# Up projections of a feed-forward layer as three rounded matmuls, with weights split on the chip and streamed through a ring of four blocks

## What is computed

```python
x = _rmsnorm(src + sa, norm1_w)
flat = x.reshape(S, C)                                   # 4096 x 256 in all
shared = _swiglu(flat @ W_shared_in) @ W_shared_out      # W_shared_in: 256 x 1024
...
h = _swiglu(flat @ W1_shared)                            # W1_shared: 256 x 1024
routed = jnp.zeros_like(shared)
for e in range(E):                                       # 8 experts, 512 x 256 each
    routed = routed + h @ W2_experts[e] * w[:, e:e + 1]  # w: gates, top 2 of a group of 4
out = x + (shared + routed).reshape(Bb, Tt, C)
```

## Time and profile before

| | |
|---|---|
| runs, median of 3 | 2171.25 us (2167.96 to 2177.17) |
| profiled execution, its own time | 2162.3 us |
| span of its trace | 2160.3 us |
| PE busy | 1944.1 us (90%) |
| DVE busy | 1376.3 us (64%) |
| ACT busy | 824.8 us (38%) |
| POOL busy | 345.0 us (16%) |
| mean granted PE clock | 0.922 of 2.4 GHz |
| DMA, mean | 48 GB/s |

### The profile page before, as it was taken

How to read it: one execution, slowest core, us unless ns; L and a number is a source line. 1 busy time by engine, 2 the same in 40 slices (tenths; PEclk the granted TensorE clock), 3 DMA queues, 4 the chain that set the end, 5 groups by cost and what they waited for, 6 DMA issues and landing times.

```text
span 2160.3 us, 31763 instructions
## 1 busy us (share of the span) xinstructions
PE 1944.1 (90%) x9200; PEld 1039.4 (48%) x9200; DVE 1376.3 (64%) x4293; ACT 824.8 (38%) x1714; POOL 345.0 (16%) x647
## 2 busy tenths in 40 slices
PE   6868899999999999999999999999999989999896
PEld 4343445536364453645455353553635445364555
DVE  7457564766857476675767657675585856767354
ACT  2433534262433425244342543426243352533410
POOL 3224013101320014100131011310122001410000
PEclk9577889999998999999999898999999998999998
DMA  5004002110030102101021010311003010110302
GB/s 178 2 20 157 1 2 98 41 41 11 7 142 1 52 1 89 60 2 51 2 89 59 10 42 2 109 40 41 12 2 115 33 51 1 70 69 2 127 10 98
DMA packets 23089, 104.69 MB, mean 48 GB/s; under 512 B 3312, under 2 KB 14192, under 8 KB 18288
## 3 DMA queue, kind: packets, MB, share of 16 engines
q1 hardware_dynamic: 21168, 89.81, 11.4%
q0 software_dynamic: 1728, 12.58, 1.5%
HBM read 84.56 MB, written 16.78 MB: 47 GB/s over the span
## 4 chain that ended last, share of the span: by engine, by line
PE 64%; DVE 17%; issue 14%; ACT 3%; POOL 1%; DVEq 0%; DMA 0%; SPq 0%; ACTq 0%; POOLq 0%
PE fb L741 14%; PE fb L719 10%; PE ot L691 9%; PE sm L649 8%; PE st L677 4%; DVE negmax L1035 3%; PE dn L617 3%; PE st L617 2%; PE st L633 2%; PE sm L677 2%; DVE acc L1228 2%; DVE sm L1032 2%; PE dn L659 1%; PE ot L617 1%; PE dn L703 1%
## 5 line engine op out<-in xcount | busy, mean ns | idle before, releaser
L538 ACT ACTIVATE probs<-st 128x512 f32<-128x512 f32 (+3 forms) x832 | 397.7, 506 | 388.2 <-PE st L677 383.5
L741 PE MATMUL fb<-w_r,h_r 128*128 128x512 f32 x1536 | 451.0, 430 | 24.7 <-DVE acc L1228 13.3
L649 PE MATMUL sm<-k_t,q_t 48*128 48x512 f32 (+3 forms) x864 | 329.1, 469 | 69.1 <-DVE negmax L1032 28.5
L741 PEld LDWEIGHTS fb<-w_r,h_r 128*128 128x128 f32 x1536 | 282.3, 197 | 137.7 <-issue 69.7
L1035 DVE TENSOR_REDUCE negmax<-sm 128x1 f32<-128x512 f32 x416 | 270.3, 686 | 105.9 <-PE sm L649 105.6
L677 PE MATMUL st<-q_t,k_t 64*128 64x512 f32 (+3 forms) x832 | 310.3, 460 | 16.6 <-ACT probs L538 16.3
L649 PEld LDWEIGHTS sm<-k_t,q_t 48*128 48x128 f32 x864 | 148.3, 201 | 365.8 <-DVE negmax L1032 181.0
L719 PE MATMUL fb<-xn_t,wup_s 128*128 128x512 f32 x512 | 303.3, 691 | 2.2 <-DVE sg L1206 2.0
L1032 DVE CUSTOM_DVE_ANT_0 sm<-sm,mask_qk 128x384 f32<-128x384 f32 (+1 forms) x448 | 203.9, 463 | 140.2 <-PE sm L649 137.7
L691 PE MATMUL ot<-probs,v_s 128*32 128x512 f32 (+3 forms) x2048 | 254.7, 537 | 2.3 <-POOL probs L441 2.3
L402 POOL TENSOR_TENSOR stack<-rot,stack 128x256 fp32r<-128x256 f32 x64 | 49.6, 775 | 1089.9 <-ACT stack L474 1089.9
(11 more groups left out here) (163 smaller groups left out, 2450.0 us busy)
## 6 DMA issues: line engine op xcount, KB each, us to landing
w_r<-w_parts SPq DMA_DIRECT2D x32, 2048.0 KB, 7.9
w_parts<-w_r POOLq DMA_DIRECT2D x4, 2048.0 KB, 8.8
x_s<-in_L_attn_query SPq DMA_DIRECT2D x8, 512.0 KB, 4.9
h_s<-in_L_ffn_W_experts POOLq DMA_DIRECT2D x8, 512.0 KB, 6.0
q_t<-rot_b SPq DMA_DIRECT2D x256, 4.0 KB
x_kept<-o_s SPq DMA_DIRECT2D x8, 512.0 KB, 3.0
xa<-x_kept SPq DMA_DIRECT2D x8, 512.0 KB, 3.7
out<-acc SPq DMA_DIRECT2D x8, 512.0 KB, 12.8
```

The lines of the kernel that those rows point to most:

```text
L538: nc.scalar.activation(probs[:, n % PSLOTS, 0:hi - lo], score_bank(m)[:, 0:hi - lo], ACT.Exp, scale=float(D) ** -0.5).then_inc(s_ex, 1)
L649: mm(max_bank(w, a)[:, 0:hi - lo], q_t[r:r + MROW, b, t * P:(t + 1) * P], k_t[r:r + MROW, b, lo:hi], start=True, stop=True).then_inc(s_sm, 1)
L741: last = mm(fb[q % 2][:, :], h_r[:, h, m, rows], w2_r[:, k % 2, w, m, :], start=(m == 0 and n == 0), stop=(m == NH - 1 and n == 2))
```

## The change

The up projections take three rounded matmuls a step in place of one in fp32. The rows get a high part (a second copy by ACT, in `stack[:, 0]`, columns 0 to 31 of each of 32 rows) and a low part (GpSimd, in `stack[:, 1]`). The weights are split by GpSimd in batch 0, `w_si` after the first attention's masks, `w1` after the second attention's low parts, through `h_s` and `h_r`, and stored to DRAM; SP streams them back each batch in eight blocks of 512 KB through a ring of four. The splitting of the first pair of expert weights moves behind them. Two of SP's first loads (1 MB each) go.

```diff
-HIDDEN_AT = spread(8 * NH - len(QUIET), 6 - LEAD, 2) + QUIET
+HIDDEN_AT = spread(8 * NH - len(QUIET), 8 - LEAD, 3) + QUIET
...
+RING = 4
...
-        wup_s = sb("wup_s", [P, 2, NC, 2 * HID])
+        wup_r = sb("wup_r", [P, RING, 2, 2, NC, P], F32R)
...
+        xn_parts = [stack[:, w, :, 0:NC * D] for w in range(2)]
...
-                (wup_s[:, 0, :, :], w_si.rearrange("(c p) n -> p c n", p=P)),
-                (wup_s[:, 1, :, :], w1.rearrange("(c p) n -> p c n", p=P)),
...
-            def place_maxima(i, a):
+            def place_maxima(i, a, f=None):
...
+                    if f is not None:
+                        for n in ((4, 5), (6,), (7,), ())[g]:
+                            load_up(f, n)
...
+            def load_up(f, n):
+
+                if n >= RING or not isinstance(f, int) or f > 0:
+                    sp.wait_ge(s_ub, f * N_UB + n - RING + 1)
+                sp.dma_start(wup_r[:, n % RING].bitcast(F32), wup_parts[n]).then_inc(s_wu[n % RING], 16)
...
                 if more:
                     sp.dma_start(x_s[:, :, :], x_v[i + 1]).then_inc(s_x, 16)
                 if f is not None:
+                    for n in range(RING):
+                        load_up(i, n)
+                if f is not None:
                     load_pair(f, 2, e)
...
             batch(0, None, None, True)
+            sp.wait_ge(s_wup, 32)
+            for n in range(RING):
+                load_up(0, n)
             sp.wait_ge(s_w2p, 16 * PAIRS)
...
             x1_from_dram(B - 2)
+            for n in range(RING, 2 * NH):
+                load_up(B - 1, n)
             store(B - 2)
...
+            def split_up(u):
+
+                pool.wait_ge(s_wur, 16 * (u + 1))
+                if u > 0:
+                    pool.wait_ge(s_wup, 16 * u)
+                for c in range(NC):
+                    raw = wup_raw[:, c].rearrange("p (h n q) -> p n h q", h=2, n=NH)
+                    g.tensor_copy(wup_split[:, :, 0, :, c, :], raw).then_inc(s_wuh, 1)
+                pool.wait_ge(s_wuh, NC * (u + 1))
+                for c in range(NC):
+                    raw = wup_raw[:, c].rearrange("p (h n q) -> p n h q", h=2, n=NH)
+                    g.tensor_tensor(wup_split[:, :, 1, :, c, :], raw, wup_split[:, :, 0, :, c, :].bitcast(F32),
+                                    ALU.subtract).then_inc(s_wul, 1)
+                pool.wait_ge(s_wul, NC * (u + 1))
+                g.dma_start(wup_parts[u * NH:(u + 1) * NH].rearrange("n p w h c q -> p n (w h c q)"),
+                            wup_split.bitcast(F32).rearrange("p n w h c q -> p n (w h c q)")).then_inc(s_wup, 16)
+
+            def rows_low(f, stacks_done):
+
+                hi, lo = (x.rearrange("p h (c d) -> p c h d", c=NC) for x in xn_parts)
+                rows = xn_t[:, :, :].rearrange("p c (h d) -> p c h d", d=D)
+                pool.wait_ge(s_sp, stacks_done)
+                for c in range(NC):
+                    pool.wait_ge(s_xh, f * N_XH + c + 1)
+                    g.tensor_tensor(lo[:, c], rows[:, c], hi[:, c].bitcast(F32), ALU.subtract).then_inc(s_xl, 1)
+
+            load_up_raw(0)
+            low_parts(0, 0)
+            mask_probs(0, None)
+            split_up(0)
+            load_up_raw(1)
+            low_parts(0, 1)
+            split_up(1)
             load_raw(0)
             load_raw(1)
             split_pair(0)
-            low_parts(0, 0)
-            mask_probs(0, None)
-            low_parts(0, 1)
             split_pair(1)
             split_pair(2)
             split_pair(3)
             with pool.Fori(1, B) as i:
                 low_parts(i, 0)
+                rows_low(i - 1, i * N_SP + 16)
                 mask_probs(i, i - 1)
                 low_parts(i, 1)
+            rows_low(B - 1, B * N_SP)
...
-            def copy_expert_rows(f):
+            def copy_expert_rows(f, i):
+                if i is not None:
+                    act.wait_ge(s_sp, i * N_SP + 12)
+                hi = xn_parts[0].rearrange("p h (c d) -> p c h d", c=NC)
                 for c in range(NC):
                     act.wait_ge(s_fp, f * N_FP + c + 1)
                     copy(xn_t[:, c, :], pair[c][:, :]).then_inc(s_fc, 1)
+                    copy(hi[:, c], pair[c][:, :].rearrange("p (h d) -> p h d", d=D)).then_inc(s_xh, 1)
...
                 if s == 0:
-                    pe.wait_ge(s_fc, (f + 1) * N_FC)
...
-                col = half * HID + m * P
-                product = mm(fb[half][:, :], wup_s[:, u, c, col:col + P], xn_t[:, c, :], start=(c == 0), stop=(c == NC - 1))
+                if s < NC:
+                    pe.wait_ge(s_xl, f * N_XL + c + 1)
+                if s % 4 == 0:
+                    pe.wait_ge(s_wu[n % RING], f * N_WU + 16 * (n // RING + 1))
+                for k, (w, x) in enumerate(((0, 0), (0, 1), (1, 0))):
+                    product = mm(fb[half][:, :], wup_r[:, n % RING, w, half, c, :], xn_parts[x][:, :, c * D:(c + 1) * D],
+                                 start=(c == 0 and k == 0), stop=(c == NC - 1 and k == 2))
```

More of the change, by code:

```diff
@@ L129, in build @@
         acc = sb("acc", [P, NT, E])
+        wup_split = h_r[:, :, :, :].rearrange("p a m t -> p (a m t)").rearrange(
+            "p (n w h c q) -> p n w h c q", n=NH, w=2, h=2, c=NC)
+        wup_raw = h_s[:, :, :].rearrange("p m t -> p (m t)").rearrange("p (c n) -> p c n", c=NC)
+        xn_parts = [stack[:, w, :, 0:NC * D] for w in range(2)]
         w2_raw = [h_s[:, :, 0:E], h_s[:, :, E:2 * E]]
@@ L235, in build @@
         s_hl, N_HL = sem("hidden_low_made"), NH
+        s_xh, N_XH = sem("expert_rows_high_made"), NC
+        s_xl, N_XL = sem("expert_rows_low_made"), NC
+        s_wur = sem("raw_up_weights_loaded")
+        s_wuh, s_wul = sem("up_weights_high_made"), sem("up_weights_low_made")
+        s_wup = sem("up_weights_stored")
+        s_wu, N_WU = [sem(f"up_weights_loaded{k}") for k in range(RING)], 16 * 2 * NH // RING
+        wup_parts = nc.dram_tensor("wup_parts", (2 * NH, P, 2, 2, NC, P), F32, kind="Internal").ap()
         w2_parts = nc.dram_tensor("w2_parts", (PAIRS, P, 2, NH, 2 * E), F32, kind="Internal").ap()
@@ L342, in batch @@
                     x1_from_dram(e)
-                place_maxima(i, 0)
+                place_maxima(i, 0, f)
                 if f is not None:
@@ L373, in _ @@
             sp.wait_ge(s_yfree, 16 * B + 16)
-        N_FIRST_LOADS, N_LOADS = 4, 15
+        N_FIRST_LOADS, N_LOADS = 4, 13
         @block.gpsimd
@@ L408, in load_raw @@
                     pool.wait_ge(s_w2l, e - 1)
+                else:
+                    pool.wait_ge(s_wul, 2 * NC)
                 g.dma_start(w2_raw[e % 2], w2[e].rearrange("(c p) n -> p c n", p=P)).then_inc(s_w2r[e % 2], 16)
@@ L451, in mask_probs, with load_up_raw @@
                                 hidden_low(f, k)
+            def load_up_raw(u):
+                if u > 0:
+                    pool.wait_ge(s_wul, NC * u)
+                g.dma_start(wup_raw, (w_si, w1)[u].rearrange("(c p) n -> p c n", p=P)).then_inc(s_wur, 16)
+            def split_up(u):
+                pool.wait_ge(s_wur, 16 * (u + 1))
+                if u > 0:
+                    pool.wait_ge(s_wup, 16 * u)
[24 more added lines that the diff above has]
+            split_up(1)
             load_raw(0)
@@ L543, in attention @@
                         if m == ROWS_FROM:
-                            copy_expert_rows(f)
+                            copy_expert_rows(f, i)
                         if m in GATE_EXPS_AT:
@@ L593, in _ @@
                 batch(i, i - 1)
-            copy_expert_rows(B - 1)
+            copy_expert_rows(B - 1, None)
             for n in range(2 * NH):
```

5 lines of the change are left out of this document (2 added, 3 removed).

## The result

The changed kernel took 2148.45 us (median of five executions, 2139.7 to 2192.31), the kernel before 2169.11 us (2163.04 to 2177.17, five on the same chip). The ratio is 0.9898, 95% interval 0.9858 to 0.9939. That is 20.7 us less where 38.7 were forecast from the terms, inside the range of 2112 to 2155 and near its upper end. Twelve more executions on another occasion had a median of 2158.82 us, above the forecast range, with a ratio of 0.9907 (0.9871 to 0.9943). By the means of all executions the changed kernel takes 0.9932 of the time before (0.9896 to 0.9971, resampled).

The account below looks back on a forecast made before the run. PE was taken to bound most of the up-projection stretch, DVE sharing its third part. Terms 26.6 + 5.6 + 2.0 + 5.0 - 0.5 = 38.7 us off gave 2132 us against the runs' median; range 2112 to 2155.

Parts of the forecast that it names:

- Start: Before the first batch: GpSimd's split no longer holds up DVE's first norm, 5.6 us gained, bounds 0 and 8.6.
- Making the rows: ACT's copies and GpSimd's subtractions for high and low rows: hidden by the later first step; uncovered, up to 3 us a batch.
- the ring: Weight blocks streamed each batch arrive in time, no cost; rival of a late block: 5 us a batch, 2167, chance 0.03.
- batch 0: GpSimd's weight splits in the first batch end near 215 us, hidden by 30 us; 0.5 us lost, bounds 0 and 4.
- the move of the spread: The lead's steps start two units later, at no cost, hiding the making of low rows by 1.5 to 2 us.
- The pieces: Moving operand in 32 pieces of 16 numbers: no cost taken; rival at half read rate, about 2269 us, chance 0.07.
- The matmuls: Up-projection steps on the chain gain 0.17 us each at full clock; 3.8 us a batch, 26.6 us over seven batches.
- the tail: Last up projections after the batches: faster steps outweigh ACT's copies, 2 us gained, bounds 0 and 5.
- the eight that DVE was to cover: Of 32 up-projection steps a batch, 8 lie behind DVE's maxima, where a faster step gives nothing.
- The clock: Half-clock drop at the lead's start gets shorter: 5 us gained, bounds 6 lost and 12 gained.
- If the half-clock stretches grow: Sign of a wrong prediction: PE's stretches at the half clock get longer than before.
- a stretch that shrinks by under 2.5 us: Sign of a wrong prediction: first to last up-projection step, about 78 us, was to get some 4 us shorter.

Follow-up runs that it names:

- e8: The changed kernel with the lead's up-projection steps spread as in the kernel before; mean 2151.8 us against the changed kernel's 2159.4.
- e5: The changed kernel with one fp32 matmul again in each up-projection step, all else kept; ratio 0.9882 to the kernel before, mean 2150.2 us.
- e3: The changed kernel with PE reading 512 contiguous numbers, the wrong rows, as moving operand of the up projections; 1993.3 us at equal clock.
- e1: The changed kernel with a fourth, low-by-low product in the eight steps of the first two head groups; 2141.91 us over ten executions, its repeat included.
- e10: e1 repeated beside the unedited changed kernel on one chip; mean time 0.9906 of that kernel's.
- e11: The changed kernel with the fourth product in steps 8 to 15, in the lead, instead of the head groups; 2143.07 us.

## Why the prediction was right, and where it was not

- **Start.** 6.6 us in the trace for the 5.6 forecast; of the same edit alone 4.3 us stay at equal clock. What the Trainium skill (SBUF — State Buffer, section SBUF: two separate sides) says of GpSimd and DVE, which stood beside it, agrees with the traces: 2.19 us with the split beside it, 0.16 without.
- **Making the rows, the ring, batch 0.** As forecast: no wait of the steps on ACT, GpSimd or a DMA. That the move of the spread was what hides the low rows is wrong: in e8, without it, they are hidden too. e5 is 5.8 us better at equal clock than the start alone explains (2029.1 against 2034.9); which of its parts gives them is open.
- **The pieces.** Not free but cheap: 0.03 to 0.04 us a step, a fifth of the exchange's 0.17, far from the 0.17 that would use it up. A run of eight misses the forecast by 0.09 us a step, mostly for another reason, which is open.
- **The matmuls.** 26.6 and 2.0 for the tail were forecast, 28.6 in all; 36.2 were found at equal clock (e5 to changed; 30 to 45 by the fit's slopes), 0.14 us for each of 256 steps. With a single step gaining 0.13, not 0.17, 36.2 is as if every step counted in full, also the eight that DVE was to cover; that they do was not tried by itself. Part of it may be the fit. The estimate of 0.21 us a step that I worked out from two pages of the Trainium skill (FP8 and Floating Point Precision, section TensorE Precision Notes; TensorE: Matmul & The Clock Gate, section Back-to-back issue gap) is not borne out: 1.13 - 1.00 = 0.13 against fp32, 0.24 for a fourth rounded product.
- **The clock: the step that failed.** Forecast 5 us gained, bounds 12 gained and 6 lost. Measured: half clock from 370 to 458 us, 32 us lost by the fit. The fall in the lead that I saw did shorten, from 10.5 to 6.8 us of half clock in the third stretch; the loss is all elsewhere. I bounded it by the later start of the lead alone. I did not ask what the same shorter steps do to a stretch that stood at the full clock with waits in it, the third row, 30.75 of 35 us busy. e5 and e3 show that the exchange causes it, e1, e10 and e11 that more load takes it back, in that stretch or in the lead. "If the half-clock stretches grow" was named as a sign of being wrong, and they grew; so was a stretch that shrinks by under 2.5 us, and on the mean of the seven it shrank by 2.2, from 77.3 to 75.1.
- **The sum.** 46.3 at equal clock less 31.7 is 14.6; the medians differ by 16.9 (17 and 59 executions) and 20.7 in the first comparison. The direction and the range held because two errors ran against each other, 13 us too little without the clock, 37 too much on it. That is luck, and it was narrow: the median of all 17 executions, 2154.41 us, is just inside the range, that of the twelve outside.

What triggers a single fall, and what ends it after 41 us, stays open: PE is 95% busy in the first half of the long low stretch (21.02 of 22.20 us) and wholly so in the second, at the same clock. That other places might avoid the falls was tried in three forms only.

The fastest version with the reference's rows and weights is e1 (and e10), the changed kernel with eight more products a batch: 2141.91 us over ten executions, 0.9916 of the changed kernel's mean (0.987 to 0.9959). e11, with 2143.07 us, is not to be told from it.

## What to carry to other kernels

When work is taken off a nearly full PE, price the clock too, in the whole batch and not only in the fall that the trace shows: give the parts where PE has waits at the full clock a bound of their own, here 0.36 us for each further us at the half clock. Compare executions by span and granted clock together; medians of a few executions mixed an effect of 46 us with one of 32 that went the other way. And if less work makes a kernel slower, try some of it back: 15 us of products bought 33 us of clock.

## What the runs showed of the hardware that was not expected

- The clock can stay at its lower level for 41 us with PE 97% busy (21.02 of 22.20 and 18.80 of 18.80 us), and at its upper level through 3.80 us with PE busy for 2.80. The Trainium skill (TensorE: Matmul & The Clock Gate, section Seeing it yourself) warns that such records are unreliable and that the gate has been seen stuck. Here the durations confirm the record, 1.65 us a step against 1.00.
- One fp32 matmul keeps the clock better than three rounded ones of the same shape: half clock 332 against 458 us, where the step took 1.12 and 1.00 us.
- A fourth rounded product costs 0.24 us in a single step, so four (1.24) are slower than the one fp32 matmul (1.13) that they replace.
- A moving operand in 32 pieces of 64 bytes costs 0.03 to 0.04 us over three matmuls of 512 columns.
